# A graph network's gathers: GpSimd waits for each block's four gathers before it starts the next four

## The chip, the cores and the metric

The kernel runs on one core of one Trainium2 chip. The metric is the device time of one execution in microseconds. Lines are given as L743: line 743 of the kernel before. Besides its compute engines (TensorE, VectorE, ScalarE, GpSimd) the core has 16 DMA engines, and each engine has a sequencer that takes its instructions in order, waits for semaphores and hands the work on.

## What is computed

Two layers over 6250 nodes of 256 features, with 100,000 edges. Cut to what matters here:

```python
# layer 0
h   = layernorm(x)
msg = h[src] + relvectors[edge_type]
red = segment_sum(msg, dst, num_segments=6250)
x   = x + gru_cell(red, h, ...)
x   = x + shared_and_top2_experts(layernorm(x))
# layer 1
xt  = layernorm(x) @ W.T + b
out = segment_sum(xt[src], dst) / (deg + 1)
x   = x + out
x   = x + top2_of_8_experts(layernorm(x))
```

The edges are sorted by dst, and dst is drawn as 6250 * u**2, so that low nodes have many more edges than high ones: the first tile of 128 nodes has 14,487 of the 100,000 edges, the last ones about 1000 each.

## The kernel before, in words

The nodes lie in 49 tiles of 128 (`NT`), the edges in 784 chunks of 128 (`CHUNKS`), four chunks to a block (`U = 4`), so 196 blocks (`BLOCKS`). The same scheme runs once in each layer.

**Gathers.** GpSimd runs `pool_chunks` (from L725). For each block it loads from `frees` how many uses TensorE must have made before the block's ring slot is free (L739), waits for that, adds one to a bookkeeping semaphore (`settled`, L142), and issues four indirect DMAs (L743). Each of these fetches 128 rows of 1 KB (512 half-precision numbers) from a table in HBM into `rows`, a ring of eight blocks (`M = 8`); the row numbers come from `srcT`. When a gather has landed, its 16 increments arrive on one of four semaphores, `landed[i % 4]`. The local function `ready` waits for the landing of a block's four gathers and adds one to `rows_ready` (L736), on which TensorE waits. In the kernel before, block i - 1 is signalled after the gathers of block i have been issued. There is one pass over the 196 blocks in each layer, written out in full; only the outer loop over passes is a loop.

**One-hots.** VectorE makes for each block a 128 x 512 matrix of zeros and ones (`dve_onehots_of`, L772) in a ring of eight of its own, and in layer 0 the one-hots of the edge types beside the rows (L782).

**Windows.** TensorE runs `pe_window` for each of the 49 tiles, from the highest to the lowest: for each block that holds edges of the tile it waits for one-hots and rows and runs eight matmuls (L811), the last of which adds one to `used`, on which both GpSimd and VectorE wait for a free slot. A block at the seam of two tiles is used by both, so that TensorE has 244 such turns in each layer for 196 blocks. The first window has three blocks; the densest tile comes last.

**The order around it.** `run_graph` (L1247) interleaves by hand, on each engine, the windows of a group of four tiles with the steps of the group before: in layer 0 the GRU and the small experts (`pe_d1` to `pe_d4` and their partners), in layer 1 the graph layer's product, normalisation and routing (`pe_e0` to `pe_e3`). While TensorE is at a step, GpSimd can fill the ring up to eight blocks and then waits for a free slot. After layer 1's graph part come the eight experts of the second feed-forward network, whose own gathers and scatters stand at L1727 and L1736.

Of the kernel before, what the change touches and what calls it, by code (L numbers as in the profile page):

```python
# [44 lines left out]
BLOCKS = CHUNKS // U  # L45
PASS = -(-(BLOCKS + M) // M) * M
# [24 lines left out]
def program(nc, a, out):  # L71
# [6 lines left out]
    with ExitStack() as ctx:  # L78
# [60 lines left out]
        def settled(eng):  # L139


            eng.sem_inc(waits_passed, 1)  # L142
# [582 lines left out]
        def pool_chunks(pool, q):  # L725

            count = pool.value_load(passes[0:1, 0:1], min_val=1, max_val=NT)
            with pool.Fori(0, count) as p:
                pool.dma_start(frees[:, :], free_after[ds(p, 1), :]).then_inc(q.frees, 16)
                pool.wait_ge(q.frees, p * 16 + 16)  # L730
                settled(pool)

                def ready(i, blocks):
                    pool.wait_ge(q.landed[i % LANDED],
                                 p * (BLOCKS // LANDED * 16 * U) + (i // LANDED + 1) * (16 * U))
                    pool.sem_inc(q.rows_ready, blocks)  # L736

                for i in range(BLOCKS):
                    pool.wait_ge(q.used, pool.value_load(frees[0:1, i:i + 1], min_val=1, max_val=NT * (PASS + 1) + MH))  # L739
                    settled(pool)  # L740
                    for s in range(U):
                        k = i * U + s
                        nc.gpsimd.indirect_dma_start(  # L743
                            out=rows[:, k % (M * U), 0:ROW], out_offset=None, in_=q.table,
                            in_offset=bass.IndirectOffsetOnAxis(srcT[:, k:k + 1], axis=0)).then_inc(q.landed[i % LANDED], 16)
                    if i > 0:
                        ready(i - 1, 1)
                ready(BLOCKS - 1, 1 + PASS - BLOCKS)

        def dve_onehots(dve, q, t, late):  # L750

# [539 lines left out]
        with nc.Block() as block:  # L1291
            @block.gpsimd
            def _(pool):
                pool_chunks(pool, q1)

            @block.tensor
            def _(pe):
                pe.sem_inc(q1.used, MH)
                run_graph(lambda g, i: pe_windows(pe, q1, g, i, BANKS1),
                          [lambda g, w, f=f: f(pe, g, w) for f in (pe_d1, pe_d2, pe_d3, pe_d4)] + [nothing], pe)  # L1300

            @block.scalar
            def _(act):
                act.sem_inc(S["hi_done"], CREDIT)
                act.sem_inc(S["lo_done"], CREDIT)

                act.dma_start(spare[:, 0:1], zeros[:, 0:1], allow_slow_non_contiguous=True).then_inc(S["table2_out"], 16)
                run_graph(lambda g, i: act_emptied1(act, g, i),
                          [lambda g, w, f=f: f(act, g, w) for f in (act_d1, act_d2, act_d3, act_d4, act_d5)], act)
                act.wait_ge(S["table2_out"], 16 * (LAST + 2))  # L1310

            @block.vector
            def _(dve):
                chain = Chain(dve, "layer0_chain", 64)
                for at in (G_ONE, G_AGAIN + E0):
                    nc.vector.memset(gate_rows[:, :, at:at + 1].bitcast(F32), 1.0)

                normalised(dve, 0, 1)
                run_graph(dve_gather(dve, q1, None),
                          [lambda g, w, f=f: f(dve, chain, g, w) for f in (dve_d1, dve_d2, dve_d3, dve_d4, dve_d5)], dve)  # L1320
# [234 lines left out]
        with nc.Block() as block:  # L1555
            @block.gpsimd
            def _(pool):

                nc.gpsimd.iota(from_list[:, :], pattern=[[1, LCOLS]], base=0,
                               channel_multiplier=0).then_inc(R["cols_ready"], 1)  # L1560
                nc.gpsimd.iota(to_list[:, :], pattern=[[0, LCOLS // SUB], [1, SUB]], base=2 * NPAD + 1,
                               channel_multiplier=SUB).then_inc(R["spares_ready"], 1)
                pool_chunks(pool, q2)
# [387 lines left out]
```

## Time and profile before

| | us |
|---|---|
| median of 3 runs | 3987.14 |
| lowest and highest | 3972.49, 4001.89 |
| the profiled execution, its span | 4051.2 |
| its busy time: TensorE | 2468.4 (61%) |
| VectorE, ScalarE, GpSimd | 1525.7 (38%), 778.7 (19%), 1836.0 (45%) |
| layer 0, gathers | from 142 to 1902 |
| layer 1, gathers | from 1968 to 3239 |
| experts and output | from there to the end |

The profiled execution has no time of its own beside its span, from the first to the last instruction; it is 1.6% above the median of the runs without a profile. An engine is busy while it executes; register, branch, semaphore and DMA-issuing instructions are not counted. A name with a q (POOLq) is the engine's sequencer. A DMA_INDIRECT of POOL is the time in which GpSimd makes the transfer's descriptors, not the transfer.

### The profile page before, as it was taken

How to read it: one execution, taken by the hardware profiler on the slowest of the kernel's cores; microseconds unless marked ns; L12 is line 12 of the kernel's file. 1: busy time of each engine (PE TensorE's matmuls, PEld its weight loads, DVE VectorE, ACT ScalarE, POOL GpSimd, SP SyncE). 2: the span in 40 equal slices, each digit the busy share in tenths (PEclk: the TensorE clock that was granted, in tenths of full speed). 3: DMA queues.
4: the chain of work that ended last, by engine and by line, in shares of the span. 5: the costliest groups of instructions: out<-in, count | busy, mean ns of one | idle time of the engine just before them, and what ended most of it. 6: DMA issues, size and time to landing. Idle time of an engine off the chain costs nothing. (4 is left out here: it accounts for less than half of the span.)

```text
span 4051.2 us, 54160 instructions
## 1 busy us (share of the span) xinstructions
PE 2468.4 (61%) x13318; PEld 1805.0 (45%) x13319; DVE 1525.7 (38%) x3970; ACT 778.7 (19%) x1414; POOL 1836.0 (45%) x2044
## 2 busy tenths in 40 slices
PE   1177776766665556444366555555444369999992
PEld 1055454544343334322234333333222159999992
DVE  6344343333333223221244443333232145555545
ACT  1122222221111112100101000000000034444441
POOL 0343333344334544455455556565666624444441
PEclk7578887777776767666567776766666579999996
DMA  4321111122212221222322223232323322112215
GB/s 131 93 59 58 54 55 44 49 63 60 60 49 62 80 64 58 64 79 70 81 84 83 79 82 91 77 89 86 91 86 88 91 72 64 63 63 63 62 43 204
DMA packets 157828, 303.02 MB, mean 75 GB/s; under 512 B 47365, under 2 KB 91816, under 8 KB 157752
## 3 DMA queue, kind: packets, MB, share of 16 engines
q0 software_dynamic: 85984, 234.74, 19.9%
q1 hardware_dynamic: 40876, 36.11, 2.9%
q10 hardware_dynamic: 30892, 31.40, 2.4%
q14 instruction: 57, 0.47, 0.0%
q8 instruction: 19, 0.31, 0.0%
HBM read 261.73 MB, written 40.39 MB: 75 GB/s over the span
## 5 line engine op out<-in xcount | busy, mean ns | idle before, releaser
L743 POOL DMA_INDIRECT rows<-table,srcT x1568 | 1534.0, 978 | 1504.4 <-PE bank L811 942.0
L811 PE MATMUL bank<-rows,onehot 128*128 x3904 | 791.3, 335 | 734.5 <-issue 597.4
L811 PEld LDWEIGHTS bank<-rows,onehot 128*128 x3904 | 422.2, 108 | 1095.6 <-issue 960.5
L772 DVE SCALAR_TENSOR_TENSOR onehot<-iota_row,tbase,dstT 128x512 f16 x488 | 367.2, 753 | 995.2 <-issue 555.6
L1773 PE MATMUL bank<-xe_high,W_high 128*128 128x256 f32 x864 | 252.5, 292 | 30.4 <-DVE xe_low L1851 30.1
L1774 PE MATMUL bank<-xe_low,W_high 128*128 128x256 f32 x864 | 250.6, 290 | 0.0
L1775 PE MATMUL bank<-xe_high,W_low 128*128 128x256 f32 x864 | 250.2, 290 | 0.0
L1773 PE MATMUL bank<-W_high,hid_high 128*128 128x256 f32 x864 | 248.3, 287 | 0.0
L1823 ACT ACTIVATE hid<-bank,b 128x256 f32<-128x256 f32 x432 | 181.6, 472 | 346.3 <-PE bank L1775 345.6
L1775 PE MATMUL bank<-W_high,hid_low 128*128 128x256 f32 x864 | 243.9, 282 | 0.0
L1774 PE MATMUL bank<-W_low,hid_high 128*128 128x256 f32 x864 | 243.8, 282 | 0.0
L1859 DVE TENSOR_TENSOR hid_low<-hid,hid_high 128x512 fp32r<-128x512 f32 x216 | 149.6, 693 | 235.0 <-ACT hid_high L1827 228.5
L1773 PEld LDWEIGHTS bank<-xe_high,W_high 128*128 128x128 f32 x864 | 171.6, 199 | 32.7 <-issue 32.7
L1462 ACT ACTIVATE sumsT<-bank 128x512 f32<-128x512 f32 (+2 forms) x28 | 13.7, 541 | 844.8 <-remote 480.1
L1774 PEld LDWEIGHTS bank<-xe_low,W_high 128*128 128x128 f32 x864 | 171.6, 199 | 0.0
L1775 PEld LDWEIGHTS bank<-xe_high,W_low 128*128 128x128 f32 x864 | 171.4, 198 | 0.0
L1727 POOL DMA_INDIRECT xs<-normal,rows_of x110 | 141.6, 1288 | 65.4 <-POOL rows_of L1723 45.8
L1774 PEld LDWEIGHTS bank<-W_low,hid_high 128*128 128x128 f32 x864 | 164.5, 190 | 0.0
L1773 PEld LDWEIGHTS bank<-W_high,hid_high 128*128 128x128 f32 x864 | 164.4, 190 | 0.0
L1775 PEld LDWEIGHTS bank<-W_high,hid_low 128*128 128x128 f32 x864 | 164.3, 190 | 0.0
L1242 ACT ACTIVATE red<-bank 128x272 f32<-128x272 f32 x49 | 19.4, 396 | 697.5 <-PE bank L814 345.7
L1736 POOL DMA_INDIRECT results<-ys,to_old x112 | 111.0, 991 | 70.7 <-POOL to_new L1717 53.6
(338 smaller groups left out, 3695.7 us busy)
## 6 DMA issues: line engine op xcount, KB each, us to landing
rows<-table,srcT POOLq DMA_INDIRECT x1568
W<-in_L_ffn_W_dram SPq DMA_DIRECT2D x14, 1024.0 KB
y<-results ACTq DMA_DIRECT2D x12, 1024.0 KB, 9.9
x_res<-in_x_dram SPq DMA_DIRECT2D x1, 6144.0 KB, 43.8
out_dram<-x_res SPq DMA_DIRECT2D x12, 512.0 KB
table<-part ACTq DMA_DIRECT2D x11, 512.0 KB
normal<-xn ACTq DMA_DIRECT2D x11, 512.0 KB
table<-part SPq DMA_DIRECT2D x6, 512.0 KB, 2.9
```

Of the source, the lines that this page charges most:

```text
L743: nc.gpsimd.indirect_dma_start(out=rows[:, k % (M * U), 0:ROW], out_offset=None, in_=q.table, in_offset=bass.IndirectOffsetOnAxis(srcT[:, ...
L772: last = nc.vector.scalar_tensor_tensor(onehot[:, ds(slot, U), :], iota_row[:, :].unsqueeze(1).to_broadcast([P, U, P]), base, dstT[:, ds(k ...
L811: last = nc.tensor.matmul(acc[:, 0:cols], hot, ring_rows[:, ds(row0 + (s * q.pitch + at), cols)], start=False, stop=False, skip_group_chec ...
L1242: nc.scalar.activation(red4[:, slot_of(g, i), :], BANKS1[i][:, 0:D + RELS], ACT.Copy).then_inc(q1.evacuated, 1)
L1462: last = nc.scalar.activation(sumsT[:, c, 0:w * P], bank[c][:, 0:w * P], ACT.Copy)
L1727: nc.gpsimd.indirect_dma_start(out=xs[:, s, :], out_offset=None, in_=normal, in_offset=bass.IndirectOffsetOnAxis(rows_of[:, s:s + 1], axis ...
L1736: nc.gpsimd.indirect_dma_start(out=results, out_offset=bass.IndirectOffsetOnAxis(to_old[:, s:s + 1], axis=0), in_=ys[:, s, :], in_offset=N ...
L1773: nc.tensor.matmul(acc, w_high, m_high, start=start, stop=False)
L1774: nc.tensor.matmul(acc, w_high, m_low, start=False, stop=False)
L1775: return nc.tensor.matmul(acc, w_low, m_high, start=False, stop=stop)
L1823: nc.scalar.activation(hid[:, hc, :], bank[1 + pair][:, o:o + TT], ACT.Gelu, bias=b1[b][:, hc:hc + 1]).then_inc(X["gelu_done"], 1)
L1859: nc.vector.tensor_tensor(hid_low[:, both, :], hid[:, both, :], hid_high[:, both, :].bitcast(F32), ALU.subtract).then_inc(X["hid_ready"], 1)
```

## The change

`ready(i)` moves from behind the gathers of block i + 1 to right behind those of block i. The last block's call, which also counts the blocks that pad the pass, becomes the last case of the same line.

```diff
--- before
+++ after
@@ -743,9 +743,7 @@
                         nc.gpsimd.indirect_dma_start(
                             out=rows[:, k % (M * U), 0:ROW], out_offset=None, in_=q.table,
                             in_offset=bass.IndirectOffsetOnAxis(srcT[:, k:k + 1], axis=0)).then_inc(q.landed[i % LANDED], 16)
-                    if i > 0:
-                        ready(i - 1, 1)
-                ready(BLOCKS - 1, 1 + PASS - BLOCKS)
+                    ready(i, 1 if i < BLOCKS - 1 else 1 + PASS - BLOCKS)
```

## Rows read from the trace of the kernel before

**Rows 1.** The page, part 5: busy, mean ns of one, idle before, its releaser.
```profile
L743 POOL DMA_INDIRECT rows<-table,srcT x1568 | 1534.0, 978 | 1504.4 <-PE bank L811 942.0
```
**Rows 2.** L743 by stretches: us, POOL busy (count), PEclk, DMA share, GB/s.
```profile
142.00:1779.00 1637.00, 681.04 (x700) 0.73 0.21 60
1779.00:1901.00 122.00, 82.15 (x84) 0.61 0.31 89
1968.00:3239.00 1271.00, 770.84 (x784) 0.66 0.30 86
```
**Rows 3.** Idle before L743 (us, times): first 142 to 1902, then 1968 to 3239.
```profile
  PE bank L811: 709.1, 48
  issue: 223.1, 713
  remote: 64.8, 21
...
  PE bank L811: 233.0, 55
  issue: 223.8, 705
  remote: 47.6, 16
  DMA rows<-table,srcT: 2.4, 8
```
**Rows 4.** Timeline of POOL, layer 1: start, us, what [idle before].
```profile
3217.57 0.95 POOL L743 DMA_INDIRECT rows<-table,srcT  x1 [0.30 <-issue]
3218.82 0.95 POOL L743 DMA_INDIRECT rows<-table,srcT  x1 [0.30 <-issue]
```
**Rows 5.** L736, L739, L142 from 3219 to 3221.5: ns min/median/max, first and last start.
```profile
L736 POOLq EVENT_SEMAPHORE  x1: 17/17/17, 3220.3 to 3220.3; - x1
...
L739 POOLq TENSOR_LOAD <-frees x1: 290/290/290, 3220.4 to 3220.4; - x1
...
L142 POOLq EVENT_SEMAPHORE  x1: 17/17/17, 3220.9 to 3220.9; - x1
```
**Rows 6.** Waits of PE, whole span: us in total, times, longest.
```profile
PE bank L811 <- issue: 597.4, 594, 7.3
...
PE bank L811 <- POOLq L736: 49.7, 29, 15.5
```
**Rows 7.** A block after a pause: timeline of POOL; L142 and L736 around it.
```profile
1895.87 1.15 POOL L743 DMA_INDIRECT rows<-table,srcT  x1 [5.78 <-remote]
...
1899.83 0.95 POOL L743 DMA_INDIRECT rows<-table,srcT  x1 [0.30 <-issue]
...
L142 POOLq EVENT_SEMAPHORE  x1: 17/17/17, 1895.1 to 1895.1; - x1
...
L736 POOLq EVENT_SEMAPHORE  x1: 17/17/17, 1902.6 to 1902.6; - x1
```
**Rows 8.** Layer 1's first block: its first and last gather (timeline) and its signal.
```profile
1968.21 0.99 POOL L743 DMA_INDIRECT rows<-table,srcT  x1 [7.37 <-issue]
...
1972.00 0.95 POOL L743 DMA_INDIRECT rows<-table,srcT  x1 [0.30 <-issue]
...
L736 POOLq EVENT_SEMAPHORE  x1: 17/17/17, 1975.6 to 1975.6; - x1
```
**Rows 9.** Timeline of PE: a block whose rows and one-hots are ready.
```profile
3049.25 1.27 PE L811 MATMUL bank<-rows,onehot 128*128 x8 [0.67 <-issue]
```
**Rows 10.** Idle before L743 from 1779 to 1901, behind the first gather's.
```profile
  issue: 24.1, 79
  remote: 15.3, 4
```
**Rows 11.** L811's register steps, 3134 to 3146 and 3149 to 3156.
```profile
L811 PEldq FUSED_REGOPS  x9: 3/700/737, 3136.3 to 3144.1; - x9
...
L811 PEldq FUSED_REGOPS  x30: 2/48/602, 3149.0 to 3155.8; - x30
```

## The prediction

> **What bounds the kernel now.** I read the page first, then the busy time by stretches, then single stretches of GpSimd and TensorE. The page shows a span of 4051.2 us in which no engine is full: TensorE is busy for 61% of it, GpSimd for 45%. Its costliest group is the one that the change touches: 1568 gathers of L743, 1534.0 us busy, 0.978 us each, with 1504.4 us of idle time in front of them, most of it ended by TensorE at L811 (a ring slot came free) [rows 1]. So GpSimd is idle between blocks for two reasons, and the sum needs them apart, by layer.
>
> The gathers run in two stretches: layer 0 from 142 to 1902 us, layer 1 from 1968 to 3239 us, 784 gathers (196 blocks) in each [rows 2]. After 3239 us GpSimd gathers for the experts by other lines, which the change leaves alone. In layer 0 the idle time before the gathers is 709.1 + 223.1 + 64.8 = 997.0 us, in layer 1 it is 233.0 + 223.8 + 47.6 + 2.4 = 506.8 us [rows 3]. Two gathers that follow each other start 1.25 us apart, 0.95 busy and 0.30 idle, at the seam of two blocks too [rows 4]. Taking 784 x 0.30 = 235 us off each stretch, and in layer 1 the 7.4 us before its first gather [rows 8], leaves the stalls: **762 us in layer 0, 264 us in layer 1**. In layer 0 GpSimd is far from bounding; in layer 1 it works 1000 of 1271 us and is the tightest engine.
>
> **What the change removes: nothing that is waited for.** Its visible aim would be an earlier signal. But the signal of a block comes early now. The last gather of one block ends at 3217.57 + 0.95 = 3218.52, and its signal (L736) is given at 3220.3, 1.8 us later, while the gathers of the next block have been running since 3218.82 [rows 4, 5]. The sequencer had already queued these four and stood at the wait. In the new order it is the same landing, 1.8 us after the same end. Only where the ring is full does the old order hold a signal back (it stands behind a free slot), and there up to seven older blocks are ready, so TensorE doesn't miss it. I count the gain at 0; its ends are 0 and the whole wait of TensorE for L736, 49.7 us [rows 6].
>
> **What it adds: a bubble at each seam.** Behind the waiting instruction on GpSimd's queue stand the signal, the load of the next limit (L739), its wait, the `settled` increment (L142) and the next four gathers; all now begin after the landing. From the end of a block's last gather to the start of the next block's first:
> - landing and signal 1.8 us. After a pause it is no shorter: the block that starts at 1895.87 after 5.78 us of idleness ends at 1899.83 + 0.95 = 1900.78 and is signalled at 1902.6, also 1.8 [rows 7].
> - signal to load to `settled`: 3220.3, 3220.4, 3220.9, so 0.6 us [rows 5]. Today this lies under the next block's gathers.
> - `settled` to the gather's start with an idle engine: 1895.1 to 1895.87, nearly 0.8 us [rows 7]. Today paid only at a stall.
> - a gather that starts on an idle engine takes 0.99 to 1.15 us instead of 0.95 [rows 7, 8]; I take 0.05 as the mean excess.
> Together 1.8 + 0.6 + 0.8 + 0.05 = 3.25 us where 0.30 stand now: **2.95 us more per block**, a block being some 5.0 us now and 7.9 to 8.0 after. The lower end is 1.5 us (the landing alone, less 0.30, the rest somehow prepared in its shade); the upper end takes the landing of the first block of layer 1, 1975.6 - (1972.00 + 0.95) = 2.65 us [rows 8], hence up to 3.8. I take 2.95 because the steady rows are nearest to what happens 390 times.
>
> By the Trainium skill (DMA: Bandwidth & Descriptors, the section on the anatomy of one SWDGE DMA) a DMA of this path takes about 2.0 us plus bytes over 436 GB/s, for 128 KB an estimated 2.3 us; the trace has 0.95 + 1.8 = 2.75 us from a gather's start to its signal [rows 4, 5]. By the page's figure the bubble would be 2.5 us and the loss in layer 1 some 220 us instead of the 311 below; the trace decides. The same page (latency and other measured facts) says that lighter memory load makes the fixed cost smaller, which would speak for cheaper landings once only one block is in flight; rows 7 against rows 5 show no such saving.
>
> **Layer 1.** 195 seams x 2.95 = 575 us more work in GpSimd's chain. The stalls that can absorb it are 264 us. The block time of 8 us lies above the 1271/196 = 6.5 us in which a block is used today, so the ring of eight is never full for long and all stalls are absorbed: **575 - 264 = +311 us**. TensorE then waits for rows at nearly every block; it needs 1.27 us and a gap of 0.67 us, 1.9 us, for one that is ready [rows 9], and one-hots are made ahead of it, so nothing else comes late. A lower granted clock in these waits costs nothing.
>
> **Layer 0.** Until 1779 us it runs 700 gathers, 175 blocks, in 1637 us [rows 2]. 175 blocks at 8.05 us are 1409 us: the stalls (709.1 us by free slots, 48 of them, nearly 15 us each for every four blocks and their 12 us of bubbles [rows 3]) cover the bubbles, and the blocks that the ring holds bridge the rest. This cover ends where the densest tile begins: from 1779.3 to 1901 run 84 gathers, 21 blocks, and after the stall ahead of the first (25.2) their idle time is 24.1 + 15.3 = 39.4 us, of which 83 x 0.30 = 25 are ordinary [rows 2, 10]. So 20 x 2.95 = 59 us meet 14.5 us of stalls: **+44.5 us**. At the very start TensorE waits for the rows of each block of the first window, which has three; the third comes two bubbles later, and the rest of the first groups follows it: 2 x 2.95, **+6 us**. Everything before 142 us, between the layers, and after 3246 us stays.
>
> **Sum:** 311 + 44.5 + 6 = 361.5 us on the profiled 4051.2, so 4413 profiled. The runs without a profile have a median of 3987.14, 0.984 of that; 361.5 x 0.984 = 356, and the forecast is 3987 + 356 = **4343 us**.
>
> **Rivals.**
> (a) Dear landings. Every block now starts from an empty queue, as the first block of layer 1 does, with 2.65 us to land [rows 8]. With 3.75 us per seam: 731 - 264 = 467, 75 - 14.5 = 60.5, and 7.5: +535, x 0.984 = 526: 4513 us. Against it: rows 7. Halfway values are likelier than the end. 15%.
> (b) Relief of TensorE. While gathers run without a break, TensorE's sequencer becomes slow: in the 12 us from 3134 to 3146 it gets through 9 register steps of L811, 0.70 us each in the median; in the 7 us from 3149 to 3156 through 30, of 0.048 us [rows 11]. If the bubbles end this, layer 0 gains. Price: L811 idles 597.4 us by "issue" [rows 6]; ordinary gaps of 0.67 us [rows 9] for its 488 turns of eight matmuls (3904) make 327, so 270 are excess, half in layer 0: -135. Layer 1 is bound by GpSimd and keeps its 311. 361.5 - 135 = 226.5, x 0.984 = 223: 4210 us; half the relief 4276. Against it: TensorE is slow for long pieces of which I can't see the trigger. 16%.
> (c) Faster than before: the same relief at L811 with a cheap seam. It decides at 217 seams (195 + 20 + 2) x s = 264 + 14.5 + 135 = 413.5, s = 1.9 us per seam. If the sequencer prepared the next block in the shade of the landing (s = 1.5), the change would be 325.5 - 413.5 = -88, x 0.984 = -87: 3900 us. Against it: load, limit and increment stand behind the wait in one in-order stream. 3%.
> (d) The stalls hide it. That holds in layer 1 only if s is below 264/195 = 1.35 us, which is below the landing alone less 0.3: about 3990 to 4005 us. The signal that comes no earlier (the change doesn't do what it says) belongs to the main case. 3%.
>
> **How the numbers follow.** Main case 63%, with 2.75 to 3.15 us per seam giving 4300 to 4386 by itself. The range takes in nearly all of (b) and half of (a): 4215 to 4455. A measurement of this kernel tells about 1% (40 us) from no change. Faster by over 1% is (c), 0.03; within 1% is (d), 0.03; slower 0.94.
>
> **What would show it right.** GpSimd's gathers in fours, 0.30 us apart inside and 3.2 to 3.3 us between blocks; "issue" or the DMA named before each fourth; busy time of L743 unchanged near 1534 us; layer 1's gathers 1270 us long now, some 1580 after, with the waits on "PE bank L811" almost gone there; layer 0 some 50 us longer, all after about 1779 us; TensorE's waits for L736 grown by hundreds of us in layer 1; the expert stage unchanged. Wrong if the gap at a seam is under 2 us or over 4 us, if layer 1 still shows long waits for free slots, or if layer 0 becomes shorter, which would be (b).

## The result, and the profile after

The changed kernel takes **4209.79 us** (median of four runs) beside 3979.81 us for the kernel before in the same comparison: a ratio of 1.0566 [1.0515, 1.0617], slower. The forecast was 4343 us in 4215 to 4455; the sign and the main mechanism held, the size did not, and the time lies 5 us below the range. (One of the four, 7966.5 us, and one of ten runs of a kernel below, 3505.1 us, lie far above the others of their kernel and are left out of the ratios but not of the medians; the other three here are 4203.57, 4208.06 and 4211.52 us.) The profiled execution has a span of 4202.0 us where its forecast was 4413. Of the four times of the kernel before, three are those that the forecast started from; the fourth, 3958.06 us, is new. From L746 on, the lines of the kernel after stand two lower, so TensorE's matmuls of L811 are L809 here.

The seam first. The costliest groups of GpSimd and of TensorE in the kernel after (busy, mean ns of one | idle before, its releasers):

```profile
L743 POOL DMA_INDIRECT rows<-table,srcT x1568 | 1522.1, 971 | 1669.2 <-issue 1606.0
L809 PE MATMUL bank<-rows,onehot 128*128 x3904 | 778.1, 361 | 1399.7 <-POOLq L736 1303.9 <-issue 44.5 <-DVE rows L780 41.9
```

Against [rows 1], the busy time of the gathers is the same, the idle time before them a little more, but its name has changed: it was "PE bank L811", a full ring, and is "issue", their own queue. TensorE's wait for the signal L736 was 49.7 us [rows 6] and is 1303.9 us. The ring has changed from nearly full to nearly empty.

The timeline of GpSimd in layer 1, and below it the three steps of the seam at 3308, as [rows 4, 5]:

```profile
3305.35 0.95 POOL L743 DMA_INDIRECT rows<-table,srcT  x1 [0.30 <-issue]
3309.49 0.94 POOL L743 DMA_INDIRECT rows<-table,srcT  x1 [3.19 <-issue]
...
3313.24 0.94 POOL L743 DMA_INDIRECT rows<-table,srcT  x1 [0.30 <-issue]
3317.39 0.94 POOL L743 DMA_INDIRECT rows<-table,srcT  x1 [3.21 <-issue]
```
```profile
L736 POOLq EVENT_SEMAPHORE  x2: 17/17/17, 3308.1 to 3316.0; - x2
...
L739 POOLq TENSOR_LOAD <-frees x1: 289/289/289, 3308.2 to 3308.2; - x1
...
L142 POOLq EVENT_SEMAPHORE  x1: 17/17/17, 3308.7 to 3308.7; - x1
```

The last gather ends at 3305.35 + 0.95 = 3306.30, the signal comes at 3308.1 (1.8 us), the bookkeeping increment 0.6 us later, the next gather 0.8 us after that: 3.19 us in all where 0.30 stood. The fourth row of the pair shows the same at the next seam. Over all seams the median is 3.23 us, and over layer 1's the mean is 3.26. The forecast's three terms 1.8, 0.6 and 0.8 are all there. Its fourth, 0.05 us for a first gather that takes longer on an idle engine, is not: the mean gather takes 971 ns, and took 978 before.

What the gathers' stretches make of it (us, GpSimd's busy time and count, clock, DMA share, GB/s), as [rows 2]:

```profile
142.00:1735.00 1593.00, 760.90 (x784) 0.75 0.24 68
1804.00:3394.00 1590.00, 761.16 (x784) 0.58 0.24 69
```

Both layers now take the same time, 196 blocks at 8.1 us: GpSimd's chain sets both. In the profiled pair the parts, measured from TensorE's first to last L811 (L809) of each layer, are:

| part | before, us | after, us | difference | forecast |
|---|---|---|---|---|
| ahead of layer 0 | 150.7 | 149.7 | -1 | 0 |
| layer 0 | 1756.7 | 1588.6 | **-168** | **+50.5** |
| between the layers | 68.7 | 73.6 | +5 | 0 |
| layer 1 | 1269.7 | 1585.7 | **+316** | **+311** |
| the rest | 805.5 | 804.4 | -1 | 0 |
| span | 4051.2 | 4202.0 | +151 | +361.5 |

The waits of the gathers of layer 1, from 1804 to 3394, as [rows 3]:

```profile
  issue: 825.2, 781
  PE bank L809: 10.1, 3
```

233.0 us of stalls for a free slot are down to 10.1, so nearly all of the 264 us of stalls (idle time beyond the 0.30 us between gathers) were absorbed as forecast, and 575 - 264 = 311 became 316. Layer 0 is another matter: it did not become longer, it became shorter, although GpSimd does 575 us more in it.

The reason stands in TensorE's sequencer. The register steps of the matmuls' line, over the whole span (ns, minimum/median/maximum), before and after:

```profile
L811 PEldq FUSED_REGOPS  x4392: 2/60/1439, 150.3 to 3245.0; - x200
```
```profile
L809 PEldq FUSED_REGOPS  x4392: 42/60/163, 149.4 to 3396.6; - x200
```

The same 4392 steps reach 1439 ns before and 163 ns after. Counted over the two layers of the trace of before and over all its steps (register steps, branches, loads), TensorE's sequencer has 602 of over 500 ns, 438 us in all, and VectorE's 392. After there are 10 and none, and the 10 are loads of a table, not register steps. TensorE's idle time by "issue" before L811 goes from 597.4 us [rows 6] to this:

```profile
PE bank L809 <- POOLq L736: 1303.9, 239, 15.1
...
PE bank L809 <- issue: 44.5, 85, 0.7
```

So with the pauses on GpSimd the slow steps of [rows 11] are gone. That is the relief of rival (b).

That the pauses drove them away is one reading of this pair. The other is that the condition behind them had passed when the kernel after ran. The new run of the kernel before at 3958.06 us, and the trace of the kernel before by itself, speak for the first. GpSimd pauses for over 2 us 116 times inside its two stretches there. The table takes the steps of TensorE's sequencer that begin while gathers follow each other, and counts them by the time since the gathers began or went on after such a pause:

| time since then, us | steps of TensorE's sequencer | over 500 ns |
|---|---|---|
| under 5 | 2798 | 24 (1%) |
| 5 to 10 | 1105 | 119 (11%) |
| 10 to 15 | 560 | 157 (28%) |
| 15 to 20 | 224 | 104 (46%) |
| over 20 | 180 | 113 (63%) |

VectorE's steps show the same: 5 of 2145 under 5 us, 109 of 1014 from 5 to 10, 132 of 361 from 10 to 15. In the kernel after, gathers run for 4.7 us as a rule and for 6.7 at most before the next pause.

The experiments ask two things: whether the seam costs what its parts say, and what the slow steps have to do with the gathers.

### The profile page after: what moved, and what is told of

It is laid out like the page before. It is cut to its first block and busy times, and to the rows that moved or that the text cites. A ratio compares the mean times of both kernels' runs of the same rounds, so it can differ in the third digit from the quotient of the medians.

```text
span 4202.0 us, 54160 instructions
## 1 busy us (share of the span) xinstructions
PE 2396.1 (57%) x13318; PEld 1809.2 (43%) x13319; DVE 1524.2 (36%) x3970; ACT 778.8 (19%) x1414; POOL 1822.8 (43%) x2044
## 5 line engine op out<-in xcount | busy, mean ns | idle before, releaser
L743 POOL DMA_INDIRECT rows<-table,srcT x1568 | 1522.1, 971 | 1669.2 <-issue 1606.0
L809 PE MATMUL bank<-rows,onehot 128*128 x3904 | 778.1, 361 | 1399.7 <-POOLq L736 1303.9
L809 PEld LDWEIGHTS bank<-rows,onehot 128*128 x3904 | 458.4, 117 | 1704.3 <-issue 1547.0
L1550 DVE TENSOR_SCALAR sums<-bank,inv_deg 128x256 f32<-128x256 f32 x49 | 23.6, 483 | 491.2 <-PE bank L812 491.2
L1725 POOL DMA_INDIRECT xs<-normal,rows_of x110 | 141.1, 1283 | 65.8 <-POOL rows_of L1721 46.3
## 6 DMA issues: line engine op xcount, KB each, us to landing
y<-results ACTq DMA_DIRECT2D x12, 1024.0 KB, 10.1
```

Source lines behind the costliest of these rows:

```text
L743: nc.gpsimd.indirect_dma_start(out=rows[:, k % (M * U), 0:ROW], out_offset=None, in_=q.table, in_offset=bass.IndirectOffsetOnAxis(srcT[:, ...
L809: last = nc.tensor.matmul(acc[:, 0:cols], hot, ring_rows[:, ds(row0 + (s * q.pitch + at), cols)], start=False, stop=False, skip_group_chec ...
L1550: nc.vector.tensor_scalar(sums4[:, slot_of(g, i), :], acc[:, 0:D], inv_deg[:, ds(tile, 1)], None, ALU.mult).then_inc(q2.evacuated, 1)
L1725: nc.gpsimd.indirect_dma_start(out=xs[:, s, :], out_offset=None, in_=normal, in_offset=bass.IndirectOffsetOnAxis(rows_of[:, s:s + 1], axis ...
```

## The experiments

The comparisons below ran later, on three chips, each with its own runs of the kernel before, and in all of these the kernel before takes **3285 to 3289 us**, not 3980. Whether the first comparison's chip is one of the three isn't recorded, so below it is "the first comparison" and "the later ones". The runs of one comparison share their kernel before. Each diff is against the kernel named. No kernel leaves any of the computation out.

**A wait a little later.** If only the wait's place matters, the wait for block i - 1 could stand between the gathers of block i. Against the kernel after, with `s` the gather's number in its block:

```diff
-                    ready(i, 1 if i < BLOCKS - 1 else 1 + PASS - BLOCKS)
+                        if i > 0 and s == 0:
+                            ready(i - 1, 1)
+                ready(BLOCKS - 1, 1 + PASS - BLOCKS)
```

> The same wait between the first and the second gather of block i. The second gather can start 2.6 us after the end of block i-1 instead of 1.55: a bubble of some 1.1 us per block, 6.1 us per block. Theory D: slow steps gone, layer 1 about 196 x 6.1 = 1200 us, in all 3750 to 3850 us. Theory P: a pause of 1.4 us between two gathers, less than half of the change's; slow steps between those of the two kernels, 3900 to 4050 us.

The same with `s == 1`:

> The wait for block i-1 and its signal stand between the second and the third gather of block i. By the steps of the prediction, landing and signal (1.8 us) and the push of the third gather (0.8 us) end 2.6 us after the last gather of block i-1, when the second gather of block i has only just ended (0.3 + 1.25 + 0.95 = 2.5 us), so there is hardly a bubble: gathers stay 1.25 us apart. Theory P (pauses: the sequencers of TensorE and VectorE take 0.7 us per step while gathers run without a pause of some us): the slow steps come back, over 400 steps above 0.5 us on TensorE's sequencer, and the time is that of the kernel before, 3960 to 4060 us. Theory D (depth: they become slow when GpSimd's sequencer has run a whole block or more ahead of its engine; a cap on what is queued cures it): under 50 slow steps, layer 1 about 1000 to 1100 us, layer 0 under 1600 us, in all 3600 to 3720 us.

And with `s == 2`:

> The same wait between the third and the fourth gather: no bubble at all, one gather more queued than in the run before. Theory P: as the kernel before, 3960 to 4060 us, over 400 slow steps. Theory D: as with the wait after the second gather, or between it and the kernel before if three queued gathers are already too many: 3600 to 3950 us.

| wait behind | us | before, us | ratio | gathers, layer 0 | layer 1 |
|---|---|---|---|---|---|
| 1st gather of the next block | 3603.61 | 3287.83 | 1.097 [1.0932, 1.1007] | 1353 | 1224 |
| 2nd | 3297.94 | 3287.83 | 1.0032 [1.0013, 1.0051] | 1259 | 1015 |
| 3rd | 3283.05 | 3287.83 | 0.9998 [0.9982, 1.0014] | 1247 | 1013 |

Behind the first gather the timeline of GpSimd shows one shorter bubble for each block:

```profile
2301.43 0.95 POOL L743 DMA_INDIRECT rows<-table,srcT  x1 [0.30 <-issue]
2303.74 0.94 POOL L743 DMA_INDIRECT rows<-table,srcT  x1 [1.36 <-DMA rows<-table,srcT]
```

1.36 - 0.30 = 1.06 us per block, named for what it is, the landing of the rows. Of the 2.93 us in the order of after, one gather ahead of the wait covers its own 1.25 us, and the 0.6 us of limit and increment now lie ahead of that gather. Two gathers cover nearly all, three everything: layer 1 takes 1224, 1015 and 1013 us, the last two about as long as before (1011). So the cost is the queue's running dry. With two gathers of lead 0.3% are left, with three nothing that can be measured. The expected times were missed by both theories in all three runs (3600 us and more for the last two), because both started from a kernel before of nearly 4000 us. Whether these orders also avoid the slow steps could not be told: the kernel before had none here to avoid.

**Layer 0 alone.** Only layer 0's pass has the new order:

```diff
+                    if q is q1:
                         ready(i, 1 if i < BLOCKS - 1 else 1 + PASS - BLOCKS)
+                    elif i > 0:
+                        ready(i - 1, 1)
+                if q is not q1:
+                    ready(BLOCKS - 1, 1 + PASS - BLOCKS)
```

> The change in layer 0 alone; layer 1 keeps the order of before. If the two layers act apart, as the two profiles say (layer 0 1757 to 1589 us, layer 1 1270 to 1586 us): the span of the changed kernel less 316, 3886 us, with slow steps in layer 1 alone. Rival: the gain of layer 0 is chance of the one profile of before (4051 us, 71 above its runs' median); then the runs lie near 3980 + 50 = 4030 us.

It took 3632.94 us, before 3287.83, ratio 1.1058 [1.1023, 1.1093]. Both expectations missed, for both started from a kernel before of nearly 4000 us. The stretches of the gathers:

```profile
143.00:1742.00 1599.00, 763.64 (x784) 0.76 0.24 68
1811.00:2825.00 1014.00, 773.79 (x784) 0.65 0.38 108
```

Layer 0 takes 1599 us, as in the first profile of the kernel after (1593), so the change in layer 0 makes it as long as it was there. What differs between the comparisons is layer 1 in the *old* order: 1014 us here, 1271 there [rows 2].

**Both kernels once more.** The kernel before and the kernel after, unchanged:

> The kernel before, profiled once more. In the last four comparisons it took 3288 us (19 runs), not the 3980 us of the first ones. Theory S (a state of the chip in which the sequencers of TensorE and VectorE take 0.7 us per step under unbroken gathers, there in the first comparison, absent in the second): without it no step of these two sequencers reaches 0.5 us inside the gather loops beyond some 10, layer 0 lasts about 1245 us and layer 1 about 1010 us, as with the wait behind the third gather; with it, the profile is that of the first run, 1757 and 1270 us. Theory W (something else in the first profile, say memory, was slow): layer 1 would be shorter at the experts too.

> The changed kernel beside the one before on the same chip. Theory S: its pauses kept the slow steps away in the first comparison, so it takes the same in either state: 4200 to 4215 us, seams of 3.2 to 3.25 us. Against 3288 that is +28%: the 2.95 us per seam are then paid in full in layer 1 (195 x 2.95 = 575 us, no stalls there to absorb them) and some 345 us in layer 0. If the changed kernel was slowed too in the first comparison, it is now well under 4200, say 3900.

Before: 3282.33 us beside 3285.02, ratio 0.9997 [0.9981, 1.0013]. After: **4206.73 us** beside 3285.02, ratio **1.2821 [1.2792, 1.285]**. The changed kernel has the same time as in the first comparison; the kernel before is 700 us faster. The profile of the kernel before, here: the register steps, then the stretches, then TensorE's waits at L811.

```profile
L811 PEldq FUSED_REGOPS  x4392: 42/60/163, 149.5 to 2482.3; - x200
```
```profile
141.00:1400.00 1259.00, 767.88 (x784) 0.85 0.30 87
1469.00:2480.00 1011.00, 770.94 (x784) 0.66 0.37 108
```
```profile
PE bank L811 <- POOLq L736: 427.9, 148, 14.9
...
PE bank L811 <- issue: 65.8, 119, 0.7
```

No register step of L811 takes over 163 ns, and "issue" is 65.8 us instead of 597.4. Nearly the whole difference of the two spans lies in the two layers of gathers: from TensorE's first to last L811 they take 1253.5 and 1006.4 us instead of 1756.7 and 1269.7, and the rest, the experts, takes 804.2 instead of 805.5, so theory W falls. The page's two queues of instruction transfers carry 57 and 19 packets in both traces, far fewer than 602, so the slow steps are not one such transfer each. Idle before the gathers, layer 0 and then layer 1:

```profile
  PE bank L811: 260.5, 38
```
```profile
  issue: 236.5, 753
  DMA rows<-table,srcT: 5.5, 18
  PE bank L811: 4.0, 13
```

In layer 1, 4.0 us of waiting for a slot are left of 233.0: GpSimd's gathers alone set the 1011 us. **Nearly all of layer 1's stalls that the forecast counted as cover are there only in the trace that has the slow steps**; in layer 0, 260.5 us of the 709.1 stay and belong to the kernel's structure. Without them the change costs 4204.0 - 3287.5 = 916.5 us of span: layer 1's gathers grow from 1010 to 1588 us, +578, where 195 x 2.95 = 575 is the price with nothing to absorb it; layer 0 grows from 1257 to 1595, +338: its idle time by "issue" grows by 556 us (230.2 to 786.2) and its stalls shrink by 211 (260.5 to 49.3).

**The block's preparation taken out of the seam.** The load of the limit, the wait for the free slot and the increment of block i + 1 move ahead of the wait for block i:

```diff
-                for i in range(BLOCKS):
+                def slot_free(i):
...
+                slot_free(0)
+                for i in range(BLOCKS):
...
+                    if i < BLOCKS - 1:
+                        slot_free(i + 1)
                     ready(i, 1 if i < BLOCKS - 1 else 1 + PASS - BLOCKS)
```

> The changed kernel with the next block's limit, its wait for a free slot and the settled increment moved ahead of the wait for the landing. If the seam is the sum of landing 1.8, registers 0.6 and push 0.8, then 0.6 us go from each: seams of 2.6 us instead of 3.2, 390 x 0.6 = 235 us less than the changed kernel, 3970 us. If the wait for the landing and the register steps overlap anyway, nothing changes.

It took 3990.43 us beside 3285.02, ratio 1.2156 [1.2128, 1.2184], 216 us less than the kernel after (expected: 3970 us). GpSimd's timeline:

```profile
2303.99 0.94 POOL L746 DMA_INDIRECT rows<-table,srcT  x1 [0.30 <-issue]
2307.54 1.10 POOL L746 DMA_INDIRECT rows<-table,srcT  x1 [2.61 <-DMA rows<-table,srcT]
```

The median seam is 2.60 us in layer 0 and 2.58 in layer 1, 0.64 less: the 0.6 us of registers, measured by taking them away. The total falls short of 235 us in layer 0: its gathers take 92 us less, layer 1's 121, where 195 x 0.64 is 125. Waits for a free slot come back there; the longest seam of layer 0 is 15 us, and 4.7 in the kernel after. What is left is landing and signal, 1.8, and 0.8 from the sequencer's push to the start on an idle engine. That part can't be prepared in the landing's shade, because the gathers themselves stand behind the wait.

**Waiting once for two blocks.**

```diff
-                    ready(i, 1 if i < BLOCKS - 1 else 1 + PASS - BLOCKS)
+                    if i % 2 == 1:
+                        ready(i - 1, 1)
+                        ready(i, 1 if i < BLOCKS - 1 else 1 + PASS - BLOCKS)
```

> The changed kernel with the wait after every second block only, for both blocks at once: 98 seams per layer with a wait, 98 without. If the cost is so many seams by 2.95 us each, layer 1 takes 1010 + 97 x 2.95 = 1296 us (1589 with all seams); layer 0, no longer bound by GpSimd throughout, 1250 + its dense end's 30 to 100 us; in all 3287 + 286 + 30 to 100 = 3600 to 3675 us. If what counts is that eight gathers follow each other or not, the cost isn't half.

3719.25 us beside 3288.72, ratio 1.1314 [1.1287, 1.134]. In the timeline eight gathers stand together, then comes the same bubble:

```profile
2008.82 0.96 POOL L743 DMA_INDIRECT rows<-table,srcT  x1 [0.30 <-issue]
2013.00 0.95 POOL L743 DMA_INDIRECT rows<-table,srcT  x1 [3.22 <-issue]
```

Layer 1 takes 1300 us: 1010 + 98 x 2.95 = 1299, so where nothing absorbs it the cost goes with the number of seams. Layer 0 grows by 142 us; I had expected 30 to 100, for I took the stalls to absorb more than they do, and so the total lies above the expected 3600 to 3675 us.

**Do the slow steps come from memory traffic?** SyncE copies 1 MB within HBM, 100 times beside layer 0's gathers and 80 times beside layer 1's, in the kernel before and in the kernel after:

```diff
+        def copies(sp, n, count):
+            for c in range(count):
+                sp.dma_start(copied[:, :], a["L1_ffn_W1"][n:n + 1, :, :].rearrange("a d h -> (a d) h")).then_inc(copy_done[n], 16)
+                sp.wait_ge(copy_done[n], c * 16 + 16)
```

> The kernel before with idle SyncE copying 1 MB of the experts' weights within HBM, one copy after the other, 100 times during layer 0's graph part and 80 times during layer 1's. If the slow steps of the first comparison are what memory pressure does to the sequencers that run loops, they come back under it: hundreds of register steps above 0.5 us on TensorE and VectorE, and layer 1 well above 1010 us. If memory pressure alone doesn't bring them, there stay some 10, and the gathers are slower only as far as the copies take DMA time: landing later, 1.25 us between gathers the same, some per cent in all.

> The same copies in the changed kernel. Its seam holds the landing, so each delay of a gather's landing by the copies is paid 392 times: with landings of 2.3 us instead of 1.8 some 200 us more than 4205 us. Before the change the same delay would be hidden (landing plus registers plus push, 3.2 us, against 5.0 us of the next block's gathers) as long as a landing stays under some 3.5 us.

| | us | before, us | ratio |
|---|---|---|---|
| copies, order of before | 3322.66 | 3285.11 | 1.0117 [1.0056, 1.0178] |
| copies, order of after | 4462.54 | 3285.11 | 1.3588 [1.3548, 1.3627] |

The page of the first has the traffic in 40 slices:

```profile
GB/s 139 152 268 245 230 240 251 247 234 89 94 95 108 108 95 109 90 138 281 267 277 279 287 169 108 108 103 109 107 105 71 68 79 55 68 68 68 43 44 239
```

The copies run beside the first part of each layer, 304 and 331 of its 784 gathers. There the traffic is 230 to 287 GB/s, nearly three times the 87 to 108 without them, and TensorE's sequencer has 12 steps of over 500 ns in both layers, all of them loads, not 602. Traffic of this kind, on a chip that shows no slow steps without it, doesn't bring them. The pair shows something else: the same copies cost the order of before 38 us and the order of after 4462.54 - 4206.73 = **256 us** (the second time from another comparison, whose kernel before agrees within 0.1 us). In the order of after each landing stands in GpSimd's chain, and under the copies a seam can look like this one:

```profile
709.97 0.94 POOL L753 DMA_INDIRECT rows<-table,srcT  x1 [0.30 <-issue]
717.50 0.94 POOL L753 DMA_INDIRECT rows<-table,srcT  x1 [6.59 <-issue]
```

The time from a gather's start to its landing is 2.7 us in the median without the copies and at most 4.1; with them it is 2.8 and at most 7.1 (minimum, median, maximum):

```profile
DMA to landing us min/median/max: 2.6/2.7/4.1
```
```profile
DMA to landing us min/median/max: 2.6/2.8/7.1
```

So it is the late ones of four that cost, not the median. The seams say the same: their median is 3.25 us with the copies as without, but 91 of the 390 are over 4 us instead of 3, and what all seams have beyond 3.3 us adds up to 267 us instead of 14. I had expected some 200 us, from landings that are longer throughout; the size was near, the way it comes about was not.

**The wait behind the third gather once more**, on another chip, in case the kernel before has the slow steps there:

> The wait behind the third gather again, to see whether the chip of this comparison shows the slow steps. If the kernel before takes 3288 us, this takes the same within 0.5%; if the kernel before takes some 3980 us, theory P says 3980 and theory D 3290 to 3400 us.

3289.59 us beside 3288.72, ratio 0.9998 [0.9984, 1.0013]. The kernel before had no slow steps here either, so this repeats the first answer and tells nothing more.

## Why the prediction was right and wrong

**The seam: right.** 3.25 us was forecast and 3.23 is the median. Three of its parts are found one by one in the timeline, one of them was taken away by itself (0.64), and only the 0.05 us of a slower first gather didn't come. Where the Trainium skill (DMA: Bandwidth & Descriptors, the anatomy of one SWDGE DMA) gives an estimated 2.3 us for this transfer, the traces have 2.6 to 2.7 us from start to landing; by the estimate from its figure layer 1 would have lost some 220 us, and it lost 316.

**No gain from the earlier signal: right.** A block's signal comes 1.8 us after the end of its last gather in both orders, and TensorE's 49.7 us of waiting for it became 1303.9.

**Layer 1: right**, +316 for +311. But the 264 us of stalls in it depended on the slow steps. Without the slow steps layer 1 of before has 4 us of them, and the same edit costs 578.

**Layer 0: the step that failed.** "+44.5" and "+6" stood there; -168 came. The cover argument (stalls of 762 us take in the bubbles) took the layer's 1757 us as given: TensorE's turns would take as long as before. They didn't; the slow steps went away, and the layer took the 1589 us of GpSimd's chain, 196 blocks at 8.1 us. This was rival (b), priced at 135 us of relief; what came is 50.5 + 168 = 218.5 us. Its price was too low by one row: I took 327 us of the 597.4 us of "issue" as ordinary, 488 gaps of 0.67 us. In the trace after all that remains is 44.5 us in 85 gaps, so 553 us were excess, 281 of it in layer 0 (318.3 before, 36.9 after). One gap of 0.67 us read from one place of the timeline [rows 9] had been multiplied by all turns. With 281 instead of 135 the price would have been too high, for it leaves out the other limit: without slow steps the layer takes the kernel before 1253.5 us, but with the bubbles GpSimd's chain stops the gain at 1589.

**The base: a second error.** I scaled 4413 by 0.984, because the profiled execution lies 1.6% above the median of the runs. The runs after are at 4204 to 4212 us and the profiled one is one of them, so nothing was to be scaled there. The kernel before spreads over 1.1% in the first comparison (3958 to 4002 us, and 4051 profiled) and over 0.6% in the later ones. That the slow steps vary from run to run is the likely reason, but only one execution with them has a trace. A factor of the kernel before was put on a kernel that doesn't have it, and by luck it hid part of the first error: 4343 is 133 us too high, 4413 is 203. The sum in profiled time misses by 4413 - 4202 = 211 us: 218.5 by layer 0, -5 by layer 1, -5 between the layers, 2 at the ends. The measured 4209.79 agrees with rival (b)'s 4210 only because its too small relief and the wrong factor cancel.

**Rivals.** (a), dear landings: fell, the seams are steady; with copies beside them it comes true in part, +256 us. (c) and (d) fell with the seam's 3.23 us. (b) came, with its layer 0 at GpSimd's limit, and [rows 11] had shown its mechanism; what I held against it, that the trigger can't be seen, spoke against knowing its size, not against its coming.

**What is shown of the slow steps, and what is not.** Shown: in the first comparison the order of before has 602 of them on TensorE's sequencer and takes 3980 us, in the later ones it has 10 and takes 3285 to 3289; the order of after has as few in both and takes 4204 to 4210. The 764 us between the two profiled spans of the kernel before lie in the gathers' layers, and within the one trace with slow steps hardly any begins in the first 5 us of gathers after a pause. Argued from this, not shown by an experiment: that the slow steps make the whole difference, and that the pauses of 3.2 us are what kept them away. No run has the slow steps and shorter or rarer pauses, so it is open too whether the pause counts (theory P) or how far GpSimd's sequencer has run ahead (theory D). Gathers without a break aren't enough by themselves: in the later profile of the kernel before they run for up to 251 us with no gap over 1 us, and no register step of L811 is slow. Not shown either: what brings the condition about, whether it belongs to a chip or to a time, whether shorter pauses (a wait behind the second or third gather) keep them away, and how the gathers slow another engine's sequencer. One guess, traffic in memory alone, was tried and fell.

## What to carry to other kernels

A wait on a landing in the stream of the engine that issues the next transfers costs landing plus restart each time (here 1.8 + 0.6 + 0.8 us against 0.30); put it two transfers further back, where it cost 0.3% here, or three, where no cost could be measured. Before stalls are booked as cover for added work, ask what makes them: here a large part came with another engine's slow register steps, which weren't there in the kernel after, and in the later comparisons they are all but gone from layer 1. And when the profiled execution lies outside the scatter of the runs, find what scatters before scaling a forecast by it; a change of what bounds the kernel changes that factor too.

## What the runs showed of the hardware that was not expected

- The same program takes 3980 us in one comparison and 3285 to 3289 us on three chips later, with equal matmul durations (335 ns mean at L811 in both); what differs in the traces is register steps of TensorE's and VectorE's sequencers, 602 and 392 of them slow, most about 0.70 us long. The kernel after shows no such difference (4209.79 and 4206.73 us).
- In the trace that has them, 24 of 2798 steps of TensorE's sequencer are slow in the first 5 us of gathers after a pause of over 2 us, and 157 of 560 from 10 to 15 us on. In the later comparisons gathers without a break didn't bring them, and neither did copies at up to 287 GB/s.
- GpSimd's restart from idle has a steady price: 0.8 us from the increment behind the wait to the start of the descriptor work (3308.7 to 3309.49 here, as in [rows 7]; 0.77 to 0.78 us at nine in ten of the seams of the kernel after), and a wait for landing and signal of 1.8 us, with one block in flight or with two.
- Copies on the queue of another engine lengthen the landing of single gathers from at most 4.1 to 7.1 us and leave the median nearly where it was, 2.7 and 2.8 us.
